# The count build: zeros written by ScalarE in place of TensorE's clearing products, and five PSUM banks instead of four

## The reference, cut to what matters

```
agg = jax.ops.segment_sum(h[src], dst, num_segments=n) / deg
h = jax.nn.relu(agg @ W_agg[l] + h @ W_self[l] + b_hid[l])
```

## Time and profile before

| | us |
|---|---|
| median of 3 runs | 7610.15 (7608.11 to 7611.19) |
| the profiled execution's own time | 7667.53 |
| its span in the trace | 7665.8 |
| count build, first product to last (L1498) | 100.6 to 1003.8 |
| ACT busy over the span | 1651.3 (22%) |
| PE busy over the span | 6321.0 (82%) |
| mean granted TensorE clock | 0.886 |

### The profile page before, as it was taken

How to read it: one execution, slowest core, us unless ns; L and a number is a source line. 1 busy time by engine, 2 the same in 40 slices (tenths; PEclk the granted TensorE clock), 3 DMA queues, 4 the chain that set the end, 5 groups by cost and what they waited for, 6 DMA issues and landing times.

```text
span 7665.8 us, 108469 instructions
## 1 busy us (share of the span) xinstructions
PE 6321.0 (82%) x29032; PEld 4993.3 (65%) x29033; DVE 3412.8 (45%) x9453; ACT 1651.3 (22%) x4349; POOL 2239.8 (29%) x2541
## 2 busy tenths in 40 slices
PE   5877799999999999766676765999999966777677
PEld 3555477778887777655555554777787755555555
DVE  7766666661111222355555566122233324444443
ACT  1344410000000111111111113132233332222222
POOL 1000010001001111366666652000111116666664
PEclk8887799999999999878877887999999988878887
DMA  4566777788779777533333336988977753333332
GB/s 138 181 228 242 256 284 261 256 299 312 273 277 343 262 257 256 184 83 83 85 82 84 83 90 200 333 291 294 354 249 244 243 181 97 102 100 99 100 100 75
DMA packets 606869, 1525.79 MB, mean 199 GB/s; under 512 B 72808, under 2 KB 248915, under 8 KB 606612
## 3 DMA queue, kind: packets, MB, share of 16 engines
q1 hardware_dynamic: 472803, 1129.19, 41.8%
q0 software_dynamic: 133824, 393.46, 17.0%
HBM read 1206.47 MB, written 316.80 MB: 199 GB/s over the span
## 4 chain that ended last, share of the span: by engine, by line
PE 59%; DVE 11%; another core or an unknown queue 11%; issue 8%; DMA 6%; DVEq 2%; ACT 2%; SPq 1%; POOL 0%; ACTq 0%; POOLq 0%
PE psum L1352 33%; PE psum L1498 4%; PE psum L1198 4%; PE psum L1646 3%; PE psum L1618 2%; PE psum L1549 2%; DMA slab<-adj 2%; DVE hot_j L2309 2%; DVE acc L2547 2%; DMA g_own<-own_dram 2%; PE psum L1630 1%; PE psum L1537 1%; PE psum L1193 1%; PE psum L1286 1%
## 5 line engine op out<-in xcount | busy, mean ns | idle before, releaser
L1352 PE MATMUL psum<-X,slab 128*128 128x512 f32 x12495 | 3111.2, 402 | 74.9 <-DMA slab<-adj 41.3
L1352 PEld LDWEIGHTS psum<-X,slab 128*128 128x128 f32 x12495 | 2347.7, 191 | 608.5 <-DVE g_x L2374 89.7
L2547 DVE TENSOR_TENSOR acc<-acc,psum 128x264 f32 (+1 forms) x1660 | 702.8, 423 | 1068.8 <-PE psum L1646 353.0
L1498 PE MATMUL psum<-hot_j,hot_key 128*128 128x392 bf16 x1592 | 570.9, 431 | 164.2 <-DVE hot_j L2309 109.4
L1012 POOL DMA_DIRECT2D table<-s_tab x147 | 80.4, 547 | 1910.8 <-DVE s_tab L2065 1910.8
L1537 PE MATMUL psum<-node_tabs,onehot_t 128*128 x1660 | 274.7, 305 | 378.3 <-ACT onehot_t L1822 348.2
L1537 PEld LDWEIGHTS psum<-node_tabs,onehot_t 128*128 128x128 f32 x1660 | 274.0, 248 | 420.6 <-issue 414.3
L1102 POOL DMA_INDIRECT ring<-gat_table,idx_slot x420 | 415.7, 990 | 261.2 <-ACT idx_slot L1817 138.1
L1102 POOL DMA_INDIRECT ring<-rel_table,idx_slot x420 | 412.6, 982 | 250.2 <-ACT idx_slot L1817 137.7
L1723 ACT CAST staged<-psum 128x392 fp32r<-128x392 f32 x808 | 373.0, 489 | 522.3 <-PE psum L1498 497.0
L1498 PEld LDWEIGHTS psum<-hot_j,hot_key 128*128 128x128 bf16 x1592 | 235.7, 148 | 321.7 <-issue 236.2
(11 more groups left out here) (426 smaller groups left out, 8124.2 us busy)
## 6 DMA issues: line engine op xcount, KB each, us to landing
slab<-adj SPq DMA_DIRECT2D x383, 1344.0 KB, 6.7
slab<-adj SPq DMA_DIRECT2D x313, 896.0 KB, 6.2
adj<-staged SPq DMA_DIRECT2D x808, 196.0 KB, 1.9
X<-table SPq DMA_DIRECT2D x32, 1792.0 KB, 13.4
table<-s_tab POOLq DMA_DIRECT2D x196, 256.0 KB, 3.5
g_own<-own_dram POOLq DMA_DIRECT2D x35, 896.0 KB, 8.1
own_dram<-s_out POOLq DMA_DIRECT2D x196, 128.0 KB, 5.1
acc<-zero_rows SPq DMA_DIRECT2D x2, 6600.0 KB, 27.4
```

The lines of the kernel that those rows point to most:

```text
L1352: last = nc.tensor.matmul(sums_of(j), slab[:, slab_at(c), u, j * P:(j + 1) * P], X[:, x_at(p, d), :], start=(d == 0), stop=(d == KT - 1))
L1498: nc.tensor.matmul(psum[:, bass.ds(own, 1), 0:J].rearrange("p o j -> p (o j)"), hot_key[:, s % KEYS // AT_ONCE, :, s % AT_ONCE], hot_j[:, ...
L2547: V.tensor_tensor(a, a, psum[:, bank, 0:w], ALU.add).then_inc(sem("summed"), 1)
```

## The change

The clearing products go. ACT writes zeros into the bank itself: a copy of `zero_j`, a table of zeros in SBUF of 128x392 fp32, into the 392 columns of the bank, which raises `evicted`. The copy out of the bank now raises a semaphore of its own, `taken`. For each part ACT does the copy out of that part's bank and then zeros the bank of the part before it, for which it waits until that part's copy is complete. Ahead of the first part it zeros all five banks.

RING is 5, LEAD is 5. PE waits before each product until `evicted` has reached z; with five zeroings ahead, this lets part z begin once part z - 5 has been zeroed, which ACT does right after the copy of part z - 4. The number of the next part is put into its register between this wait and the product. PE loads the registers twice a turn as before. ACT's loop goes over five octets of parts at a time, since the ring of five comes round only after 40 parts; each octet still loads its eight registers. SP waits for `taken` in place of `evicted`.

```
-    RING = 4
-    LEAD = RING - 1
+    RING = 5
+    LEAD = RING
 ... (PE)
-                    z = pe.snap(zs[s % NOW], min_val=1, max_val=LEAD + ENDED)
+                        z = part_of(s)
                     if s % 4 == 0:
                         pe.wait_ge(*ev("hot", t * BUILD + (s + 4)))
+                    pe.wait_ge(sem("evicted"), z)
                     own = (z % RING).with_bounds(min_val=0, max_val=RING - 1)
+                    if s + 1 < steps and (s + 1) % NOW > 0:
+                        z = part_of(s + 1)
                     nc.tensor.matmul(... hot_key ..., hot_j ..., start=False, stop=True, ...).then_inc(sem("meet_mm"), 1)
-                    pe.wait_ge(sem("evicted"), z)
-                    next_own = ((z + 1) % RING).with_bounds(min_val=0, max_val=RING - 1)
-                    cleared(psum[:, bass.ds(next_own, 1), J:J + 2].rearrange("p o j -> p (o j)"))
...
+            pe.wait_ge(*ev("taken", ENDED))
             pe.wait_ge(*ev("evicted", LEAD + ENDED))
 ... (ACT)
+            def zeroed(bank):
+                nc.scalar.copy(psum[:, bank, 0:J], zero_j[:]).then_inc(sem("evicted"), 1)
...
-                    nc.scalar.copy(staged[:, r, :], psum[:, (r + 1) % RING, 0:J]).then_inc(sem("evicted"), 1)
+                    nc.scalar.copy(staged[:, r, :], psum[:, (turn * AT_ONCE + r + 1) % RING, 0:J]).then_inc(sem("taken"), 1)
+                    if not (isinstance(i, int) and r == 0):
+                        act.wait_ge(*ev("taken", i * AT_ONCE + r))
+                        zeroed((turn * AT_ONCE + r) % RING)
...
+            for z in range(1, RING + 1):
+                zeroed(z % RING)
...
-            with act.Fori(1, OCTETS) as i:
-                parts_evicted(i)
+            with act.Fori(0, OCTETS // RING) as i:
+                for m in range(1, RING + 1):
+                    parts_evicted(i * RING + m, m % RING)
+            act.wait_ge(*ev("taken", ENDED))
+            zeroed(ENDED % RING)
 ... (DVE)
-            V.memset(carrier[:, 7:8], 0.0).then_inc(sem("evicted"), LEAD)
+            V.memset(zero_j[:], 0.0).then_inc(sem("zero_j"), 1)
-            V.tensor_copy(iota_k[:], iota_row[:])
```

More of the change, by code:

```diff
@@ L205, in build @@
             at_now = COLS + 2 * T
-            iota_k = node_tabs[:, at_now:at_now + P // 2].bitcast(BF16)
             edge_now = node_tabs[:, at_now + P // 2:at_now + P // 2 + BUILD]
@@ L278, in build @@
                 staged = sb("staged", [P, AT_ONCE, J], F32R, scope=late)
+                zero_j = sb("zero_j", [P, J], scope=late)
         with ExitStack() as scope:
@@ L505, in build @@
                              ("cuts", 1), ("bound_read", 1), ("cuts_read", 1), ("z_rows", 1), ("parts_out", 1), ("marks", 1), ("x_ve", 1), ("more_rows", 1),
-                             ("b_self", 1), ("rows2_f", 2), ("x_rstd", 1), ("chunk_i", 1), ("edge_f", 2), ("turn_row", 1), ("w_att", 2 * Q),
+                             ("b_self", 1), ("rows2_f", 2), ("x_rstd", 1), ("chunk_i", 1), ("zero_j", 1), ("edge_f", 2), ("turn_row", 1), ("w_att", 2 * Q),
                              ("amax", 1), ("gdiag", 1), ("dst_tab", 1), ("zs_clamped", 1), ("bn_ve", 1), ("bn_shift", 1),
@@ L729, in parts_out @@
                 for r in range(AT_ONCE):
-                    sp.wait_ge(*ev("evicted", i * AT_ONCE + (LEAD + r + 1)))
+                    sp.wait_ge(*ev("taken", i * AT_ONCE + (r + 1)))
                     to = sp.snap(to_regs[r], min_val=0, max_val=PARTS + MORE - 1)
@@ L1483, in _, with part_of @@
             zs = [pe.alloc_register(f"pe_part{n}") for n in range(NOW)]
-            def cleared(bank_ap):
-                nc.tensor.matmul(bank_ap, iota_k[:], iota_k[:, 0:2], start=True, stop=True, skip_group_check=True)
+            def part_of(s):
+                return pe.snap(zs[s % NOW], min_val=1, max_val=LEAD + ENDED)
             def build(t, steps):
@@ L1507, in _ @@
             pe.wait_ge(*ev("step_part", 16))
-            pe.wait_ge(*ev("hot", 1))
-            cleared(psum[:, 1, J:J + 2])
             by_meets(pe, build, 2)
+            pe.wait_ge(*ev("taken", ENDED))
             pe.wait_ge(*ev("evicted", LEAD + ENDED))
@@ L1712, in _, with parts_evicted @@
                     nc.scalar.copy(by_step[:, f:f + count, :], psum[:, n, 0:count * P].rearrange("p (s c) -> p s c", c=P)).then_inc(sem("rows2_T_read"), 1)
+            def zeroed(bank):
+                nc.scalar.copy(psum[:, bank, 0:J], zero_j[:]).then_inc(sem("evicted"), 1)
             last_regs = [act.alloc_register(f"act_last{r}") for r in range(AT_ONCE)]
-            def parts_evicted(i):
+            def parts_evicted(i, turn=0):
                 act.load(last_regs, part_last[0:1, bass.ds(i * AT_ONCE, AT_ONCE)])
@@ L1720, in parts_evicted @@
                     act.wait_ge(sem("meet_mm"), act.snap(last_regs[r], min_val=1, max_val=MEETS))
-                    if not isinstance(i, int):
+                    if not (isinstance(i, int) and i == 0):
                         act.wait_ge(*ev(f"staged_out{r}", i * 16))
-                    nc.scalar.copy(staged[:, r, :], psum[:, (r + 1) % RING, 0:J]).then_inc(sem("evicted"), 1)
+                    nc.scalar.copy(staged[:, r, :], psum[:, (turn * AT_ONCE + r + 1) % RING, 0:J]).then_inc(sem("taken"), 1)
+                    if not (isinstance(i, int) and r == 0):
+                        act.wait_ge(*ev("taken", i * AT_ONCE + r))
+                        zeroed((turn * AT_ONCE + r) % RING)
+            act.wait_ge(*ev("zero_j", 1))
+            for z in range(1, RING + 1):
+                zeroed(z % RING)
             act.wait_ge(*ev("part_rows", 32))
+            assert OCTETS % RING == 1
             parts_evicted(0)
-            with act.Fori(1, OCTETS) as i:
-                parts_evicted(i)
+            with act.Fori(0, OCTETS // RING) as i:
[3 more added lines that the diff above has]
+            zeroed(ENDED % RING)
             act.wait_ge(*ev("steps_T", 1))
```

## The result

The changed kernel takes 7510.3 us (7506.46 to 7525.1, 4 runs) against 7610.67 for the kernel before: ratio 0.9873, 95% interval 0.9859 to 0.9888.

The account below looks back on a forecast made before the run. The prediction took PE's sequencer to bound the count build, with ACT taking over in its last two thirds. Terms of -45, -6 and +5 us summed to -46, from 7610 to 7565 us, range 7530 to 7612.

Parts of the forecast that it names:

- A: First third of the count build, 571 products in about 300 us before; forecast to gain 45 us.
- B: Second third of the count build, 529 products and 304 parts in 300 us; forecast to gain 6 us.
- C: Last third of the count build, 495 products and 308 parts in 304 us; forecast to lose 5 us.
- the term of 45 us for A: First third: PE saves 0.10 us a meet, 57 us over 571, of which four fifths were taken; bounds 27 and 57.
- 0.22 us between products: PE at the high clock: product spacing falls from 0.36 to 0.22 us, bounds 0.18 and 0.28.
- rival 2: Count build: with fewer products PE's clock stays low at 1.2 GHz; about 7606 us, no change; chance 0.11.
- ACT's 0.91 us per part: ACT, each part: copy 0.40, zeroing 0.40 and 0.105 for the octet's end, making ACT the bound in B and C.
- The end of an octet at 0.84: ACT's register load every eight parts: 1.24 us extra, 0.40 covered by a zeroing, leaving 0.84, or 0.105 a part.
- The ring's full state: C: full four or five times in each of 15.5 turns, 0.40 us each, 28 us against 24 of room.
- Rival 1: B and C: ACT becomes the bound; without overlap 1.085 us a part, 15 us slower, 7625 us; chance 0.12.
- Rival 3: PE: the bank's number makes spacing 0.28 us; A gains 27, 24 us faster in all, 7586 us; chance 0.12.
- Rival 4: B and C: the ring is no hindrance, each gains 15 us; 75 us faster in all, 7535 us; chance 0.15.

Follow-up runs that it names:

- e4_halves_after: Changed kernel with hot_j made by two DVE operations of 196 columns in place of one of 392: ratio 0.9967 to the kernel before.
- e5_halves_before: Kernel before with hot_j made by two DVE operations of 196 columns in place of one of 392: ratio 1.0000 to the kernel before.
- e11_computation: Changed kernel with a longer bank number computation, (z + RING) % RING in place of z % RING: ratio 0.9860 to the kernel before.
- the control: Changed kernel itself, run again unaltered beside other follow-up runs because chips differ: ratio 0.9869 to the kernel before.
- e3_ring4: Changed kernel with RING and LEAD of 4 in place of 5: ratio 0.9967 to the kernel before.
- e2_product: Changed kernel with a 128x128 by two columns product put back ahead of every meet's product, reusing the computed bank number: ratio 0.9991.

## Why the prediction was wrong

The direction and the place were right: most of it in A, little in B. C gained 5 us where 5 were to be lost. The mechanism was right in that PE's clearing pair was the price before and ACT's work and the ring hold B and C after. Two terms of the sum were mis-sized, and after the change it is no longer PE that is late in A.

**The failed step is the term of 45 us for A.** It measured 72, beyond the 57 that I had called its bound, and it rested on PE staying the later engine ("DVE does not cap it outright"). In its place the runs show that DVE's work sets A: 0.398 us a meet against DVE's own 0.37, and 56 of 71 us of added DVE work went into A (e4_halves_after), none in the kernel before (e5_halves_before).

How the term came about, step by step. First, it took 0.22 us between products and called 0.18, half of the old spacing, the least possible; measured is 0.166. The old spacing was the sequencer's, and half of its instructions is not half of its time: the trace of the change and e11_computation put what is left at about 0.17. Second, it held the share of time at the high clock at 68%, though I argued in rival 2 that the array would be less idle; A was granted 0.94, so 88% high. With the measured figures a meet needs 0.88 x 0.166 + 0.12 x 0.33 = 0.19 rather than 0.26, and the saving against 0.36 is 97 us, more than DVE leaves room for. Third, it took a fifth off for the tie with DVE. The better sum was to go by the other engine: DVE's 210 us and a little for its start, not a share of PE's saving. The earlier trace rows had that number, 214.74.

One figure in it was right by luck. 328 ns, the shortest product, was taken for the low clock and gave 0.345 between products; measured is 0.33. In the trace of before, the products that run wholly at the low clock take 501 ns at least, and those of 328 are all at the high one. The 0.36 of the earlier trace rows, too, was read at the low clock for the high one; it holds there all the same (140.55 to 141.28 us above).

**ACT's 0.91 us per part** was 0.80. The two copies at 0.40 each were right, also that a source in SBUF and a target in PSUM change nothing (medians 498 and 511 ns against 489 in the earlier trace rows); the lower bound of 0.36 for a zeroing has no row behind it, and no run shows it. The end of an octet at 0.84 was wrong: measured 0.05 in the rows above and 0.12 in the median. The 1.24 us of the earlier trace rows was no plain load either: the load took 1.07 of it, a branch of the loop came before it, and the copy's own product ended only 0.27 us before the copy began. The change runs that branch once in five octets. And with work always queued, ACT's sequencer runs the load ahead: at the octet end shown above the load began at 797.02, before the octet's last copy had. So ACT needed 612 x 0.80 = 490 us of the 604 in B and C, not 557, and there was room for 114. Only 22 of these were had, 16 in the control. What holds the rest is, for the most part, the ring with PE's stops: a bank more gave 35 us, shorter stops 28, both 41 against the control.

The ring's full state was priced at 28 us in C, at four or five times a turn and 0.40 us each. Measured are 59.0 us of PE's waiting for zeroings in C in 86 times, so 5.6 times a turn and 0.69 each. And I had no price for the fifth bank itself; e3_ring4 puts it at 50 us in B and C.

Rival 1, ACT at over 1.06 us, fell: the alternation overlaps fully. Rival 2, the low clock, fell in A (0.94 against 0.84) and not in C (0.72 against 0.76). The Trainium skill's rule that activity releases the throttle ("TensorE: Matmul & The Clock Gate", "What's actually happening") agrees with A: the products that count came 2.5 to the us, where they came 1.9. C does not settle it: 1.66 to the us against 1.63, while PE's idle time grew from 68 us to 81. Rival 3, a dearer computation of the bank's number, fell: 87 ns for the new instruction against 94 and 98 to 100 for the two of before, and e11_computation. Rival 4, the ring being no hindrance, was nearest in time and wrong as a mechanism: the ring still hinders, and B and C gained 22 us, not 30. Nothing moved outside the stage: passes one to three took 2142 us, against 2143.

Of the saving between products at the high clock, the queued ones show the array's part, 0.23 to 0.166 us, and the others the sequencer's, 0.36 to 0.17. A product with a sequencer instruction of 43 ns is some 0.13 us of the latter (e2_product: 0.30 against 0.17). Left open: what each of the two takes by itself, why loads of four were worse than loads of eight, and what sets B and C beyond ACT's work, the ring and the stops.

## What to carry to other kernels

When work is taken from the engine that is late, don't take a share of its saving: the new time is the need of whichever engine comes next, and that can be read in the profile before (DVE's busy time per meet was 0.365 to 0.376 us in every third, before and after). A gap that an idle engine shows at a register load or a loop's end is not a cost that an engine with work queued behind it will pay (0.12 us in the change; 0.60 where ACT had to wait for its own copy). And work that is handed to an engine which feeds a ring of buffers costs by slack as much as by time: here one bank was worth 72 us, the order of two copies 70.

## What the runs showed of the hardware that I had not expected

One more product of 128x128 by two columns per meet, with one more sequencer instruction of 43 ns, made the stage 83 us longer over 1592 meets, 0.05 us each on average and 0.09 in the third that PE can delay. Adding a term to an address computation within one instruction cost 9 to 10 ns, and the same again in the spacing of products where none were queued. Register loads on PE go by the number of registers, 0.11 us each (16: 1.8 us, 8: 0.9, 4: 0.5 in the mean). A zeroing by ACT from SBUF to PSUM, alternating with a copy out of PSUM, starts every 0.40 us, as copies alone do.
